# Who rounds the first experts' weights, and who fills a bias row: a mixture-of-experts block on one core

## What is computed

```python
x = x + tanh(g_xattn) * attention(layernorm(x), ctx)        # V = ctx @ Wv + bv, among others
h = layernorm(x)
e = argmax(h @ router_w.T, axis=-1)                          # one of 8 experts a token
# for the tokens of expert e, I = 704:
g, u = h @ gate_w[e].T, h @ up_w[e].T
x = x + tanh(g_ffn) * ((silu(g) * u) @ down_w[e].T)
```

## Time and profile before

| | us |
|---|---|
| median of 3 runs | 192.47 |
| lowest and highest | 191.69, 193.42 |
| the profiled execution, as timed | 193.59 |
| its span, first to last instruction in the profile | 191.6 |
| PE busy | 173.2 (90%) |
| POOL busy | 127.6 (67%) |
| DVE busy | 126.6 (66%) |
| ACT busy | 118.1 (62%) |

### The profile page before, as it was taken

The page is one execution under the profiler, slowest core; times in us unless marked ns, Lnnn a source line. Parts: engine busy times, 40 slices in busy tenths (PEclk is TensorE's granted clock), DMA queues, the critical chain, the costliest instruction groups (busy, mean ns, idle before and its releaser), DMA issues.

```text
span 191.6 us, 4426 instructions
## 1 busy us (share of the span) xinstructions
PE 173.2 (90%) x1387; PEld 158.5 (83%) x1387; DVE 126.6 (66%) x340; ACT 118.1 (62%) x286; POOL 127.6 (67%) x119
## 2 busy tenths in 40 slices
PE   6999979999795669998999999999999999999960
PEld 3657668998694559997998899999999899999950
DVE  1379358888998517644897596595595698645720
ACT  0557749765889429886837778566887906604500
POOL 4000479999424799998898898898898994105021
PEclk9999999999999999999999999999999999999996
DMA  5999733634940312997219718509702101001010
GB/s 157 340 348 364 277 123 111 195 127 156 318 171 1 94 38 57 399 323 254 66 32 343 229 32 338 211 18 344 242 4 62 58 29 35 28 3 56 3 37 29
DMA packets 11855, 29.00 MB, mean 151 GB/s; under 512 B 2072, under 2 KB 8681, under 8 KB 10790
## 3 DMA queue, kind: packets, MB, share of 16 engines
q1 hardware_dynamic: 6738, 20.46, 31.2%
q0 software_dynamic: 1920, 4.53, 7.5%
q10 hardware_dynamic: 3156, 3.48, 5.2%
HBM read 24.26 MB, written 4.52 MB: 150 GB/s over the span
## 4 chain that ended last, share of the span: by engine, by line
PE 65%; POOL 9%; DMA 8%; issue 7%; DVE 6%; ACT 2%; ACTq 1%; POOLq 0%
PE ps L1259 27%; PE ps L1292 19%; POOL wgu L562 5%; DMA both<-in_ctxT 4%; PE ps L1122 4%; PE ps L1044 4%; DMA xin<-x_rows,table 3%; PE ps L1107 3%; PE ps L1144 3%; PE ps L1095 2%; POOL xin L630 2%; PE ps L1237 1%; DVE x L1416 1%; PE ps L1133 1%; DVE MT L1440 1%
## 5 line engine op out<-in xcount | busy, mean ns | idle before, releaser
L1259 PE MATMUL ps<-xhT,wgu 128*128 128x256 f32 (+2 forms) x528 | 68.7, 288 | 2.1 <-DVE xhT L1567 1.3
L1259 PEld LDWEIGHTS ps<-xhT,wgu 128*128 128x128 f32 x528 | 66.5, 188 | 3.5 <-issue 2.2
L562 POOL TENSOR_TENSOR wgu<-raw_gu,wgu 128x1408 fp32r<-128x1408 f32 (+1 forms) x22 | 52.4, 2402 | 0.2
L1292 PE MATMUL ps<-wd,hT 128*128 128x256 f32 (+1 forms) x340 | 43.1, 284 | 0.5 <-DVE hT L1593 0.2
L1292 PEld LDWEIGHTS ps<-wd,hT 128*128 128x128 f32 (+1 forms) x340 | 40.8, 180 | 1.7 <-DVE hT L1593 0.8
L639 POOL DMA_INDIRECT out<-xin,table x20 | 20.2, 1009 | 24.5 <-DVE xin L1606 21.0
L1584 DVE TENSOR_TENSOR ps<-V_all,ps 128x336 f32<-128x336 f32 x40 | 20.5, 512 | 24.0 <-PE ps L1259 11.0
L630 POOL DMA_INDIRECT xin<-x_rows,table x20 | 21.6, 1078 | 7.6 <-issue 4.1
L934 ACT ACTIVATE V_all<-ps 128x336 f32<-128x336 f32 x40 | 17.8, 445 | 8.8 <-PE ps L1259 8.3
L800 ACT ACTIVATE wgu<-raw_gu 128x704 fp32r<-128x704 f32 (+2 forms) x31 | 20.8, 746 | 1.5 <-issue 0.9
L1593 DVE TENSOR_TENSOR hT<-ps,hT 128x336 fp32r<-128x336 f32 x40 | 20.1, 502 | 0.4
(11 more groups left out here) (168 smaller groups left out, 239.6 us busy)
## 6 DMA issues: line engine op xcount, KB each, us to landing
raw_gu<-in_Wgu SPq DMA_DIRECT2D x8, 1408.0 KB, 6.8
both<-in_Wd SPq DMA_DIRECT2D x8, 640.0 KB, 4.3
xin<-in_x SPq DMA_DIRECT2D x7, 256.0 KB, 9.0
x_rows<-x ACTq DMA_DIRECT2D x7, 256.0 KB, 2.2
both<-in_WdL SPq DMA_DIRECT2D x16, 64.0 KB, 4.7
both<-in_ctxT ACTq DMA_DIRECT2D x2, 480.0 KB, 9.0
xin<-x_rows,table POOLq DMA_INDIRECT x20, 5.8
out<-xin,table POOLq DMA_INDIRECT x20
```

Source lines behind the costliest of these rows:

```text
L562: pool.tensor_tensor(lo[where], raw[where], hi[where].bitcast(F32), ALU.subtract)
L1259: last = pe.matmul(ps[:, bank, 0:n], weights(j, w_part, c, i, kind), xhT[:, j % 2, x_part, c, 0:n], start=(c == 0 and (w_part, x_part) == ...
L1292: last = pe.matmul(y_of(j, k), hT[:, h_part, some], wd[:, j % SPLIT, i, w_part, :], start=(s == 0 and n == 0 and (k % 2 == 0 or j == E - 1 ...
```

## The change

Three things are changed.

1. **The bias row of V.** VectorE fills `V[96:P]` itself, just before its first `context`, and there are 2 slots in place of 4, so the fill is 32 partitions by 528 elements in place of 1056. `p_vb` is gone. ScalarE writes the router's part of `bvb` ahead of `norm1(2)` in place of behind it.
2. **Expert 1's low gate and up weights.** TensorE makes them in four pieces (`low_first`). A piece is two pairs of matmuls of 352 columns: the identity times the raw weights (fp32), and a negated identity times their high part (fp32r), summed in PSUM; ScalarE copies the sum out (`low_first` there, L851 and L853). Two pieces stand between the counting and the table, where 20 of the 80 spins are left, and two behind L1223, where 8 of the 56 are left. ScalarE makes the negated identity (`negative`) ahead of its last statistics.
3. **Expert 2's gate and up weights.** GpSimd makes both parts (`own_gu(SPLIT - 1, 1)`: two casts, a small one, and the differences) at the place where it made the low parts of experts 1 and 2. ScalarE no longer makes expert 2's high part. `HAND_GU` is 2, and the waits of `p_lg` and `a_hg` are recounted in `high_gu_done` and `low_gu_done`; SyncE's load of expert 3 waits for `a_lg` (expert 1's four copies) in place of `p_lg`.

```diff
-SLOTS = 4
+SLOTS = 2
-HAND_GU, HAND_D = 1, 2
+HAND_GU, HAND_D = 2, 2
...
+        minus = xhT[:, 1, 0, 0, 0:P]
...
+        def high_gu_done(eng, j):
+
+            if j == 1:
+                eng.wait_ge(a_hg, 1)
+            elif j >= SPLIT:
+                eng.wait_ge(a_hg, j + 1 - HAND_GU)
+
+        def low_gu_done(eng, j):
+
+            if j == 1:
+                eng.wait_ge(a_lg, 2 * C)
+            else:
+                eng.wait_ge(p_lg, j if j else 1)
...
-                    if j - RAW >= HAND_GU:
-                        sp.wait_ge(a_hg, j - RAW + 1 - HAND_GU)
-                    sp.wait_ge(p_lg, j - RAW + 1)
+                    high_gu_done(sp, j - RAW)
+                    low_gu_done(sp, j - RAW)
...
-            pool.wait_ge(d_bv, 16)
-            pool.wait_ge(a_tg, 2)
-            pool.wait_ge(a_u, 2)
-            pool.tensor_scalar(V[96:P], bvb[96:P].unsqueeze(1).to_broadcast([P - 96, SLOTS, W]), tgn[96:P, 0:1], None,
-                               ALU.mult).then_inc(p_vb, 1)
-            pool.wait_ge(p_vb, 1)
             pool.wait_ge(v_guess1, 1)
...
-            low_gu(1, 1)
-            low_gu_chunk(SPLIT - 1, 0, 1)
-            low_gu_chunk(SPLIT - 1, 1, 1)
+            own_gu(SPLIT - 1, 1)
             gather_full(AHEAD)
...
+            def negative():
+
+                act.activation(minus, ident[:], ACT.Copy, scale=-1.0).then_inc(a_ng, 1)
+
+            def low_first(n):
+
+                c, o, bank = n // 2, n % 2, 6 - 2 * (n % 2)
+                act.wait_ge(t_lg, n + 1)
+                ins = act.activation(halves(1, 1, c)[:, :, o, :], ps[:, bank:bank + 2, 0:HALF], ACT.Copy)
+                if o:
+                    ins = act.activation(tails(1, 1)[:, c, :], ps[:, bank + 1, HALF - LAST:HALF], ACT.Copy)
+                ins.then_inc(a_lg, 1)
...
             scored(2)
-            norm1(2)
             act.wait_ge(t_u, 2)
             act.activation(bvb[:, H:W], ps[:, 7, 32:32 + E], ACT.Copy).then_inc(a_u, 1)
+            norm1(2)
...
-            high_gu(1, 0, 2)
+            high(raw_of(1, 0), halves(1, 0, 0)).then_inc(a_first, 1)
+            negative()
             statistics(B - 1)
...
             ins.then_inc(a_lo, 1)
+            low_first(0)
+            low_first(1)
             high_gu(1, 1, 2)
-            split_first_gu(SPLIT - 1)
...
             sizes = [count(act, 0)]
+            low_first(2)
             act.wait_ge(v_stat, 1)
             for k in range(FULL):
                 gathered(0, k)
             turned_x(0)
+            low_first(3)
...
+            def low_first(n):
+
+                c, o, bank = n // 2, n % 2, 6 - 2 * (n % 2)
+                if n == 0:
+                    pe.wait_ge(a_first, 1)
+                    pe.wait_ge(a_ng, 1)
+                elif n == 1:
+                    pe.wait_ge(v_x1, B)
+                else:
+                    pe.wait_ge(a_hg, 1)
+                    pe.wait_ge(a_lg, n - 1)
+                for s in range(2):
+                    pe.matmul(ps[:, bank + s, 0:HALF], ident[:], raw_of(1, c)[:, s, o, :], start=True, stop=False)
+                    last = pe.matmul(ps[:, bank + s, 0:HALF], minus, halves(1, 0, c)[:, s, o, :], start=False, stop=True)
+                last.then_inc(t_lg, 1)
...
-            spin(80)
+            low_first(0)
+            low_first(1)
+            spin(20)
...
-            spin(56)
+            low_first(2)
+            low_first(3)
+            spin(8)
...
+            pe.wait_ge(a_lg, 3)
             turn_x(0, sizes[0])
             spin(16)
             for j in range(E):
-                pe.wait_ge(p_lg, j + 1)
+                low_gu_done(pe, j)
...
             dve.wait_ge(a_tg, 2)
-            dve.wait_ge(p_vb, 1)
+            dve.wait_ge(d_bv, 16)
+            dve.wait_ge(a_u, 2)
+            link(dve.tensor_scalar(V[96:P], bvb[96:P].unsqueeze(1).to_broadcast([P - 96, SLOTS, W]), tgn[96:P, 0:1], None, ALU.mult))
             context(0)
```

More of the change, by code:

```diff
@@ L287, in flamingo_moe @@
         d_gu, d_d = [sem(f"d_gu{j}") for j in range(E + RAW)], [sem(f"d_d{j}") for j in range(E + RAW)]
-        a_hg, a_hd = sem("a_hg"), sem("a_hd")
-        p_lg, p_ld, v_ld = sem("p_lg"), sem("p_ld"), sem("v_ld")
+        a_first, a_hg, a_hd = sem("a_first"), sem("a_hg"), sem("a_hd")
+        p_lg, t_lg, a_lg, a_ng, p_ld, v_ld = sem("p_lg"), sem("t_lg"), sem("a_lg"), sem("a_ng"), sem("p_ld"), sem("v_ld")
         k_pool = sem("k_pool")
@@ L304, in flamingo_moe @@
         t_wr, v_wrc, v_ax = sem("t_wr"), sem("v_wrc"), sem("v_ax")
-        t_wvt, a_wvt, t_u, a_u, p_vb = sem("t_wvt"), sem("a_wvt"), sem("t_u"), sem("a_u"), sem("p_vb")
+        t_wvt, a_wvt, t_u, a_u = sem("t_wvt"), sem("a_wvt"), sem("t_u"), sem("a_u")
         v_vr = sem("v_vr")
@@ L555, in low_gu_chunk @@
             def low_gu_chunk(j, c, pieces):
-                if j >= HAND_GU:
-                    pool.wait_ge(a_hg, j + 1 - HAND_GU)
+                high_gu_done(pool, j)
                 raw, hi, lo = raw_of(j, c), halves(j, 0, c), halves(j, 1, c)
@@ L603, in own_d, with own_gu @@
                 low_d(e, 3)
-            def own_gu(e):
+            def own_gu(e, pieces):
                 pool.wait_ge(d_gu[e], 16)
@@ L610, in own_gu @@
                 link(pool.tensor_copy(tails(e, 0), raw_tails(e)))
-                low_gu(e, 4)
+                low_gu(e, pieces)
             own_d(0)
-            own_gu(0)
+            own_gu(0, 4)
             own_d(1)
@@ L704, in run @@
                 if j == E:
-                    pool.wait_ge(p_lg, E)
+                    pool.wait_ge(p_lg, E - 1)
                     pool.iota(iota_x[:].rearrange("p t (e k) -> p t e k", e=MORE), pattern=[[0, NTOK], [NTOK, MORE], [1, BL]], base=0, channel_multiplier=0, **fl)
@@ L835, in statistics @@
                 act.activation(mv2[:, t, 1], sums, ACT.Copy, scale=1.0 / H).then_inc(a_var, 1)
-            def split_first_gu(e):
-                act.wait_ge(d_gu[e], 16)
-                for part in range(2):
-                    high_gu(e, part, 2)
+            def negative():
[7 more added lines that the diff above has]
+                ins.then_inc(a_lg, 1)
             act.wait_ge(t_wqbk, 1)
@@ L1244, in turn_rest @@
                         pe.wait_ge(v_xhT3, j)
+                    if j == 0:
+                        pe.wait_ge(a_lg, 2 * C)
                     pe.wait_ge(a_xh3, j + 1)
```

## The result

The changed kernel takes 188.2 us, the median of 4 executions (186.19 to 189.74), the kernel before 192.66 beside it (191.69 to 193.42): a ratio of 0.967, 95% interval 0.961 to 0.973. Run three more times, on three chips, it gave 0.971 (0.966 to 0.977), 0.974 (0.967 to 0.982) and 0.969 (0.962 to 0.975); the median of all its 22 executions is 187.9. Forecast were 187.4 and 186.1 to 190.2, so the sum holds. Ratios leave disturbed executions out (of the four, 189.28 and the profiled 189.74, in which the granted clock was lower than in the two others), medians don't, so that the two can differ by some tenths of a per cent.

A forecast was written before the change was run, and what follows sets the result against it. The prediction took TensorE's chain as the bound, with gains only where the chain steps off TensorE, four places here. Its terms, 1.45 + 0.95 + 1.5 + 1.2 = 5.1 us, took the median of 192.47 to 187.4, range 186.1 to 190.2.

The forecast's parts named there:

- The bias row: Before the first V and in the loop: VectorE's fill is hidden and GpSimd starts earlier, gaining 1.45 us (1.1 to 1.6).
- The logits: In the sort: VectorE's first product no longer stands behind GpSimd's differences, 0.27 us for 1.29, gaining 0.95 us.
- The low products: On TensorE before expert 0: pieces of 1.5 us replace spins and are covered, so counted at nothing.
- my own sign of being wrong: Before expert 0: table matmuls or expert 0's first ones waiting behind a piece would show the forecast wrong.
- Experts 1 and 2: Earlier gathers end ScalarE's waits for rows in both experts, gaining 1.5 us in expert 1 and 1.2 in expert 2.
- My yardstick for expert 2: Expert 4, with the same 256 columns, lasts 12.75 us, so expert 2's 14.10 was taken as 1.35 too many.
- Experts 3 to 7 keep their lengths: Later experts: GpSimd stays as far ahead as it was, or 1 us further, so no change was counted.
- expert 0's silence in the sum: Expert 0 had no term in the sum: its length was forecast to change by 0.
- the lower end: Range's 186.1 us: each term at its upper bound, and 0.7 of the 1.0 us in expert 5.
- The sum: Whole kernel: 1.45 + 0.95 + 1.5 + 1.2 = 5.1 us gained, from the median of 192.47 to 187.4.
- waits come back in another form: Rival, experts 1 and 2: other late things leave 1.0 us gained in place of 2.7, 189.1 us; chance 0.20.
- The clock rival: TensorE without 108 spins drops to 1.2 GHz if a hole beyond 1.34 us opens before expert 0: 195.4 us; chance 0.05.

The follow-up runs named there:

- bias: The kernel before with only the bias row's edit (2 slots, fill on VectorE, ScalarE's copy moved ahead): 190.92 us, ratio 0.990 to the kernel before.
- nobias: The changed kernel without the bias row's edit (4 slots, fill on GpSimd again): 190.18 us, ratio 0.987 to the kernel before.
- poollate: The changed kernel with three more GpSimd copies ahead of its work on expert 0's down weights: 189.86 us, ratio 0.981 to the kernel before.
- again: The changed kernel run once more without an edit, for a second profile: 187.66 us, ratio 0.971 to the kernel before.
- loadmid37b: Second run of the changed kernel with expert 3's load issued inside expert 0 and expert 7's inside expert 4: 186.96 us, ratio 0.968 to the kernel before.
- gatherlate: The changed kernel with three more GpSimd conversions ahead of its work for expert 2: 192.26 us, ratio 0.994 to the kernel before.
- loadmid: The changed kernel with expert 3's gate and up load issued some 2.2 us into expert 0: 187.12 us, ratio 0.970 to the kernel before.
- loadlate: The changed kernel with expert 3's gate and up load also waiting for GpSimd's expert 2 weights: 189.35 us, ratio 0.983 to the kernel before.
- loadmid37: The changed kernel with expert 3's load issued inside expert 0 and expert 7's inside expert 4, first run: 186.55 us, ratio 0.968 to the kernel before.
- again2: The changed kernel run once more without an edit, after its second profile: 188.04 us, ratio 0.974 to the kernel before.

## Why the prediction was right, point by point

**The bias row: right, undersized.** 1.71 measured for 1.45, and the same 22.89 in bias. The fill cost 0.49 for 0.6, and the row's new place was hidden. The chain of before that ended last shows the two parts, with what stands in place of the usual 0.89 for L1144 and 0.22 and 0.89 for L1133 and L1122:

```profile
24.45 1.13 issue
25.58 1.13 PE ps L1144 x4
...
30.93 0.29 PE ps L1133 x2
31.23 1.16 PE ps L1122 x8
```

The first is 1.13 of stop and 0.24 by which the first `values` behind it was longer, 1.37 together; the second, 0.34, lies where ScalarE's 0.7 for `nm` arrives, and was put at 0.3. nobias has both again (1.00 and 1.13, 0.29 and 1.16). What I mis-sized is the slower product behind the stop, which I had left out.

**The logits: right in mechanism, oversized.** The product lost 1.01 of the 1.02, and poollate brings the stall back. But only 0.67 of the 0.95 reached the path. I had checked what would be late behind the last residual and not what VectorE needs next: TensorE's last `values`, 0.43 late.

**The low products: right at full clock.** Pieces of 1.5 us, an idle of 0.52 left before the table, and no delay of expert 0 at full clock (17.7 with pieces, 19.6 before). The forecast of nothing here hid two things. Under a half clock the third piece takes 2.95, ScalarE's gathered rows wait for it, and some 0.3 to 0.9 come out: there my own sign of being wrong, expert 0 waiting behind a piece, was met in part. And in before's own profile ScalarE was idle for 1.18 ahead of its second gathered block with nothing that the profile shows to wait for, which no other profile has. So how much of the 1.0 by which the stretch is shorter in again is the change's stays open.

**Experts 1 and 2: right, with the second undersized.** 1.6 for 1.5, 1.75 for 1.2. My yardstick for expert 2, expert 4 with 12.75, is itself 0.4 longer than need be: in loadmid37b it lasts 12.35. The gather 9.9 us behind the last, no wait for gathered rows in either. gatherlate shows that the wait returns when the gather does. I had left VectorE 1 us of its blocked low part; it lost nearly all (5.55 to 2.67).

**"Experts 3 to 7 keep their lengths" failed, and so did expert 0's silence in the sum.** I wrote that SyncE's load of expert 3 "now goes out some 4 us earlier", and it did, by 4.3 against expert 0's start. I priced that at nothing. It costs 1.4 to 1.7 us in expert 0: loadmid and loadlate, which only delay the load, have 12.46. That it does so through TensorE's own instructions is the likely way and not shown. In expert 4, 0.7 to 3.6 are lost, and loadmid37 and loadmid37b, in which the load of expert 7 goes out later, take that back. How early the load goes out doesn't explain it alone: 1.5 us ahead of expert 4 in before, which has no stop, and 1.5 to 2.5 in the four profiles of the changed kernel, with again2, whose stop is 1.73, at 1.5. Expert 5 gave 0.9, which I had only in the lower end.

**The sum held because misses of both signs met, which is luck.** Two stops of 1.5 and 1.4 and 0.3 less in the logits stand against 0.3 more in the loop, 0.7 more in experts 1 and 2, 0.9 in expert 5 and, in the single profiles compared, 2.1 of start and sort that I can't ascribe to the change. The account isn't closed: without these 2.1 the rows of the table give 3.6 us, while the medians of the two kernels differ by 4.4 to 5.4 in the four comparisons. So 0.8 us or more of the gain is placed in no stretch. Of the rivals, "waits come back in another form" had the right kind with the wrong place: not in experts 1 and 2 but in 0 and 4. The clock rival's fall did happen, at 58 us, though no hole beyond 1.34 had opened (the longest in the 4 us ahead of it was 0.93): its condition was wrong. Nor did every longer hole bring a fall: loadlate's 3.05 us in expert 1 passed at 1.00, while 2.11 us in the first profile's expert 4 and 2.82 in poollate were followed by 0.50. The fall at 58 us cost under 1 us and is in bias as well.

## What to carry to other kernels

A release that comes earlier on one engine starts loads earlier: for every load that a change moves, name what else it will lie beside, a gather and, as it seems, the engines' own instruction blocks included. When a term removes a stall, price what its consumer needs next, not only the engine that stalled. And one profile of before is one execution: its longest odd wait may be no part of the kernel.

## What the hardware did that I had not expected

TensorE stood for 0.67 to 2.06 us in expert 0 with no semaphore to wait for, in each of the eight profiles in which a 1408 KB load was in flight as the expert began, and in none of the six in which it went out 2.5 us into the expert or later; a packet of the instruction queue came some 3 us later in the eight.

The granted clock fell to 0.50, the 1.2 GHz level, for some 3 us near 58 us in some executions of the same kernel and not in others (0.50 in the changed kernel's first profile, 0.61 in again, 1.00 in again2). In again TensorE had been busy for 0.80 of the 2 us from 54 and 0.95 of the 2 from 56. again2, with 0.83 and 1.04, kept the full clock, and so did loadmid with 1.08 and 0.76. What decides between them stays open.

In poollate VectorE got one instruction done for each of GpSimd's, so a 16-element product took 1.25 us beside a difference of 1.26.
